# VectorE's order in an attention tile: the second half's low part goes behind the next row maximum

## The reference

```python
# layer 0: linear attention without softmax, per image, x_flat is 128 x 1024
pairwise_weight = jnp.matmul(theta_x, phi_x) / N
y = jnp.matmul(pairwise_weight, g_x)
out = x_flat + _conv1x1(y, out_w, out_b)
# layer 1: softmax attention over the 1024 pixels; the values are the layer's own input
theta = conv1x1(x, theta_w, theta_b); phi = conv1x1(x, phi_w, phi_b)
scores = jnp.einsum('ncp,ncq->npq', theta, phi) / sqrt(c)
attn = jax.nn.softmax(scores, axis=-1)
f = jnp.einsum('npq,ncq->ncp', attn, g)
result = conv1x1(f, conv1_w, conv1_b);  return x + result
```

## Time and profile before

| what | value |
|---|---|
| median of 3 runs | 177.07 us |
| profiled execution, its own time | 177.18 us |
| span in that profile | 175.0 us |
| TensorE matmul busy | 167.1 us, 96% |
| VectorE busy | 132.6 us, 76% |
| ScalarE busy | 102.5 us, 59% |
| GpSimd busy | 35.9 us, 21% |

### The profile page before, as it was taken

How to read it: one execution, slowest core, us unless ns; L and a number is a source line. 1 busy time by engine, 2 the same in 40 slices (tenths; PEclk the granted TensorE clock), 3 DMA queues, 4 the chain that set the end, 5 groups by cost and what they waited for, 6 DMA issues and landing times.

```text
span 175.0 us, 2722 instructions
## 1 busy us (share of the span) xinstructions
PE 167.1 (96%) x974; PEld 137.0 (78%) x974; DVE 132.6 (76%) x190; ACT 102.5 (59%) x176; POOL 35.9 (21%) x32
## 2 busy tenths in 40 slices
PE   7799997999999999999999999999999999998994
PEld 7683685878888888968889888968888788876694
DVE  0316889897997776996987777897989689899811
ACT  3034477858673465958673374958675557656410
POOL 1106500005003100644102200544202202330000
PEclk9999999999999999999999999999999999999999
DMA  4600000003001000013001000010001000100011
GB/s 138 192 0 0 4 0 0 0 4 120 0 2 62 0 4 0 0 60 124 0 0 60 0 0 0 0 60 0 0 0 51 9 4 0 60 2 0 0 64 60
DMA packets 2537, 4.71 MB, mean 27 GB/s; under 512 B 288, under 2 KB 992, under 8 KB 2528
## 3 DMA queue, kind: packets, MB, share of 16 engines
q1 hardware_dynamic: 2096, 4.26, 7.0%
q10 hardware_dynamic: 432, 0.33, 0.7%
HBM read 2.49 MB, written 2.10 MB: 26 GB/s over the span
## 4 chain that ended last, share of the span: by engine, by line
PE 69%; DVE 13%; ACT 7%; issue 5%; DMA 4%; SPq 1%; ACTq 0%; DVEq 0%
PE ring L254 24%; PE ring L334 19%; PE turned L304 10%; DVE negmax L699 5%; DVE PT_lo L714 4%; DMA X<-x_dram 4%; ACT P L570 3%; PE ring L244 3%; PE ring L317 3%; ACT PT_hi L579 2%; PE ring L262 2%; PE ring L208 2%; PE ring L219 2%; DVE V_lo L693 1%; PE turned L208 1%
## 5 line engine op out<-in xcount | busy, mean ns | idle before, releaser
L579 ACT ACTIVATE PT_hi<-turned 128x512 fp32r<-128x512 f32 x62 | 35.9, 596 | 24.3 <-PE turned L304 24.3
L699 DVE TENSOR_REDUCE negmax<-ring 128x1 f32<-128x1024 f32 x32 | 39.1, 1220 | 13.6 <-PE ring L254 13.4
L570 ACT ACTIVATE P<-ring,negmax 128x1024 f32<-128x1024 f32 x32 | 35.8, 1119 | 21.5 <-DVE negmax L699 21.5
L714 DVE TENSOR_TENSOR PT_lo<-turned,PT_hi 128x512 fp32r<-128x512 f32 x62 | 42.1, 683 | 4.9 <-ACT PT_hi L579 4.9
L304 PE MATMUL turned<-identity,P 128*128 128x128 f32 x256 | 36.1, 274 | 2.4 <-DVE P L707 1.7
L304 PEld LDWEIGHTS turned<-identity,P 128*128 128x128 f32 x256 | 30.3, 141 | 9.4 <-DVE P L707 1.9
L707 DVE TENSOR_SCALAR P<-P,rden 128x1024 f32<-128x1024 f32 x32 | 28.5, 890 | 1.1
L334 PE MATMUL ring<-PT_hi,V_hi 128*128 128x512 f32 x56 | 23.8, 425 | 0.3
L334 PE MATMUL ring<-PT_hi,V_lo 128*128 128x512 f32 x56 | 22.1, 395 | 0.0
L334 PE MATMUL ring<-PT_lo,V_hi 128*128 128x512 f32 x56 | 22.1, 395 | 0.0
L254 PE MATMUL ring<-Phi_hi,T_hi 128*128 128x512 f32 x62 | 21.2, 423 | 0.0
(11 more groups left out here) (102 smaller groups left out, 198.3 us busy)
## 6 DMA issues: line engine op xcount, KB each, us to landing
out_dram<-result SPq DMA_DIRECT2D x7, 256.0 KB, 2.0
X<-x_dram SPq DMA_DIRECT2D x3, 512.0 KB, 3.3
X_first<-x_dram SPq DMA_DIRECT2D x2, 256.0 KB, 4.2
w<-weights_dram ACTq DMA_DIRECT2D x1, 194.0 KB, 5.6
out_dram<-result SPq DMA_DIRECT2D x1, 192.0 KB, 1.9
wi<-inner_dram SPq DMA_DIRECT2D x1, 64.2 KB, 5.9
pg_w<-pg_weights_dram ACTq DMA_DIRECT2D x1, 64.0 KB, 3.3
pg_b<-pg_bias_dram ACTq DMA_DIRECT2D x1, 64.0 KB, 5.5
```

The source lines that it names most:

```text
L570: nc.scalar.activation(P[:, t % P_BUFFERS, :], ring[:, slots[t], :], ACT.Exp, bias=negmax[:, t:t + 1], accum_out=den[:, t:t + 1]).then_inc ...
L579: nc.scalar.activation(PT_hi[:, g, half_chunks(h), k * TILE:(k + 1) * TILE], turned[:, columns(h)].rearrange("p (j r) -> p j r", j=CHUNKS_ ...
L699: nc.vector.tensor_reduce(negmax[:, t:t + 1], ring[:, slots[t], :], AX.X, ALU.max, negate=True).then_inc(max_ready, 1)
L714: nc.vector.tensor_tensor(PT_lo[:, g, half_chunks(h), rows], turned[:, columns(h)].rearrange("p (j r) -> p j r", j=CHUNKS_PER_HALF), PT_hi ...
```

## The change

On VectorE, low(t-1,1) used to stand behind norm(t). Now it stands one step of the loop later, behind max(t+2) and ahead of low(t,0). Each tile's high and low parts, their number and their sizes stay as they are, and so does the order on every other engine. The last one of the loop, low(5,1), stands ahead of norm(7), as before.

```diff
                 for t in range(TILES - 1):
                     row_max(b, t + 1, slots)
+                    if t >= 2:
+                        low_turned(b, t - 2, 1)
                     if t >= 1:
                         low_turned(b, t - 1, 0)
                     norm(b, t)
-                    if t >= 1:
-                        low_turned(b, t - 1, 1)
                     if t == 3:
                         low_v(b, V_SLOT if has_next else LAST_V_SLOT)
                         if has_next:
                             low_a(b + 1)
+                low_turned(b, 5, 1)
                 norm(b, 7)
```

## The result

The changed kernel takes 193.75 us, the median of 4 runs (193.54 to 195.44), against 177.06 (177.04 to 177.19): a ratio of 1.0961, 95% interval 1.09 to 1.1023. The forecast was 192.3, with 187.5 to 196.0 as its range. The profiled execution took 193.54 us with a span of 191.3, so its parts are measured against the profiled execution of before, 177.18 and 175.0: 16.36 us more.

A forecast was written before the change was run, and what follows sets the result against it. TensorE, busy 96% of the span, was taken as the bound. Delays of 4.15 + 4.0 + 4.0 + 3.1 = 15.25 us on the profiled 177.18 give 192.4, predicted as 192.3 us, range 187.5 to 196.

The forecast's parts named there:

- The deciding number, 1.92 us: Time from the scores' end until TensorE can go on, with a maximum and then a low part made on VectorE.
- V's parts: Before turn(3,1): values, then V's high part on ScalarE and low part on VectorE, 1.06 us later by start.
- the bound of 42.5 us: Sign of error: the prediction is wrong if a loop image stays under 42.5 us.
- The small waits: At turn(4,1) and turn(5,1): 1.84 us of work against 1.92 needed, 0.30 us each with the restart, bounds 0 and 0.5.
- the sum: Added time of the four images, 4.15 + 4.0 + 4.0 + 3.1 = 15.25 us.
- The restart: TensorE's half turn after a wait takes 0.66 us, against 0.44 in a row: 0.22 more per wait.
- pulled-ahead weight loads: Rule against the sum: weight loads done during TensorE's waits would make restarts free, some 3.5 us less.
- the clock falls: Rival, 3%: TensorE's idle waits drop its clock to 1.2 GHz for a stretch, 16 us on top, 208 us.
- signs of being wrong: Loop image under 42.5 us, waits before a norm's consumer or for V_lo instead, or granted clock below full.
- The wait for `PT_hi`: VectorE's idle time before the low part L714, said to be gone in the profile after.
- VectorE falls behind: Rival, 9%: norm(3) to norm(5) run long, low parts of tiles 4 and 5 up to 1 us late, about 197 us.
- The other side: Rival, not slower, 3%: eight maxima on VectorE come 0.6 us sooner, 4.8 us in all, 172.3 us.

The follow-up runs named there:

- fill_more: fill_all plus 14 unused matmuls between turn(1,0) and turn(1,1) of image 0; 192.08 us, ratio 1.085.
- last_tile4: The kernel before the change, with only low(4,1) of the last image put behind max(7); 176.60 us, ratio 0.9984.
- clock_fill: The changed kernel with 24 unused matmuls between turn(3,0) and turn(3,1) of the last image; 193.07 us, ratio 1.0896.
- loop_only: The changed kernel's order in images 0 to 2 only, the old order in the last image; 189.63 us, ratio 1.0706.
- fill_all: The changed kernel with unused matmuls in all eight long waits, before turn(2,1) and turn(3,1) of each image; 193.35 us, ratio 1.0893.
- two_long: The changed kernel with only low(1,1) and low(2,1) deferred, tiles 0, 3 and 4 in the old order; 192.66 us, ratio 1.0861.
- tile2: The kernel before the change, with only low(2,1) put behind the next maximum; 183.71 us, ratio 1.0387.
- values_between: The changed kernel with values, and fold_x or scores(6), moved into TensorE's two long waits, and ScalarE's order at tile 4 changed; 180.05 us, ratio 1.0194.
- tile1: The kernel before the change, with only low(1,1) put behind the next maximum; 182.02 us, ratio 1.0286.
- other_three: The changed kernel with only low(0,1), low(3,1) and low(4,1) deferred, tiles 1 and 2 in the old order; 179.76 us, ratio 1.0137.
- best: last_tile4, and in image 0 ScalarE makes high(1,1) ahead of exp(3); 176.22 us, ratio 0.9951 against the kernel before the change.

## Why the prediction was right

**The deciding number, 1.92 us.** It held in every place. With the 3.68 us by which image 1 starts later, the working put the waiting turns at 72.33, 76.67, 83.44 and 90.19; they are at 72.35, 76.55, 83.35 and 90.11. In the other images too, the waiting turns start 1.89 to 1.92 us after the scores' end by the chain of waits. Two are apart: turn(3,1), whose low part comes by way of V's parts, and turn(1,1) of image 0, where the scores were long done.

**The sizes.** A loop image takes 101.56 - 57.63 = 43.93 us by the starts of tile 7's turn in the chain of waits, forecast 44.0. For image 2 the same two marks lie 42.09 us apart and lay 38.19 apart before, so it grew by as much, 3.90 us; what tells is the growth, not the bound of 42.5 us that the prediction set for any loop image. Images 0 to 2 cost 11.52 us by the start of the last image, and 0.28 more that came back because the input landed sooner in this execution: 11.8 together, forecast 12.15, which was too high in image 0 above all (3.96 against 4.15). The small waits cost 0.28 each, taken at 0.30. The last image cost 4.84 us, of which 1.56 are the clock's; 3.3 remain, forecast 3.1. The rest is a wait of 0.17 us for the low part ahead of the last group's matmuls, at 181.75, that the sum didn't have. The two misses partly cancel.

**The restart.** The turns that waited for the deferred low parts took 0.65 or 0.66 us in the profile after, but for the one of 1.12 us at half clock, so pulled-ahead weight loads spared nothing here: the loads of the waiting transposes waited with them, as the sum assumed. This is the weight load (PEld) of turn(2,1) in image 1:

```profile
76.54 0.42 PEld L304 LDWEIGHTS turned<-identity,P 128*128 128x128 f32 x4 [1.72 <-DVE PT_lo L714]
```

**What was off.** Of the measured 16.7 us, some 1.6 are not in the sum. They come from the rival "the clock falls", to which I gave 3%, and which I priced as a drop after every pair of waits, 16 us in all. It was mis-sized in both ways. By the mean granted clocks it happened in every execution of the changed kernel, and it was small: one drop in three of them (0.991), two in the fourth (0.982, 195.44 us). A granted clock below full was one of the prediction's own signs of being wrong, and it came. The forecast that nothing but waits would come was therefore wrong as put; that 192.3 was still near 193.75 is luck in this respect, for the drop happened to be cheap. fill_more, the new order without drops, at 192.08, is what the sum describes.

**Smaller misses.** VectorE's busy time fell from 132.6 to 128.0 us, where I said unchanged; most of it is norm's L707, which took 28.5 us before and 24.7 after. The wait for `PT_hi`, said to go, is 1.6 us still, and the longest idle stretch before a turn is 2.06 us, where 1.9 was the most expected. "VectorE falls behind" did not come: its low parts run in pairs behind a maximum, and it still waits for scores ahead of the next.

**The other side.** The maxima gained nothing in the loop, since scores were not ready. That a deferral can pay where the deferred part has cover is what last_tile4 suggests (0.4 us, with an interval that reaches no change); in its profile the wait before turn(6,1) is gone.

## What to carry to other kernels

Moving work later on an engine that isn't the bound costs nothing only as long as the bound has work of its own until that result is needed. Count that work from the event that the moved instruction now stands behind (here 0.44 us against 1.92), tile by tile, since a hand-made order has a different cover at each. A long wait on TensorE can also cost it its clock for a while, here about 1.6 us each time, on top of its length.

## What the runs showed of the hardware

The granted clock can fall to 0.50, the 1.2 GHz level, after idle stretches of 1 to 2 us, and where it does so differs between executions of the same kernel. The changed kernel had it in the last image in its profile, after waits of 1.48 and 2.06 us; clock_fill, loop_only and fill_all in image 0, after waits of 0.81 and 1.06 us close together; two_long in image 2 and in the last, after 1.48 and 1.86 and after 1.48 and 2.05. Each drop took about 0.009 off the mean clock, and executions with one took 1.2 to 2.6 us longer than those without, mostly 1.2 to 1.8.

Of the kernels with waits of 1.8 us or more, the changed kernel had it in 4 of 4 executions, two_long in 4 of 4, and loop_only, clock_fill and tile2 in 2 of 4 each. Of those whose waits are shorter, fill_all had it in 4 of 6, values_between in 1 of 4, and tile1 (1.07 to 1.48 us), other_three, last_tile4, best and fill_more never, in 4, 4, 9, 5 and 5 executions. fill_all, values_between and other_three all have the pair of 0.81 and 1.06 us in image 0, so such waits make a drop possible, not certain; what decides in a given execution stays open. Between the last products before these waits and the drop, TensorE did little but half turns, that is transposes, while the fills are ordinary matmuls. Whether the kind of work matters, beside the idle time, no run here separates.

The Trainium skill, "TensorE: Matmul & The Clock Gate", section "What's actually happening", has it that the clock is gated by TensorE's recent activity. That fill_more, which adds nothing but unused matmuls, shows clock 1.000 in five of five executions agrees with it, with the reserve that it ran on another chip than fill_all.
